# An attention, mixture-of-experts and projection kernel on eight cores: the projection's first block is split, most of it ahead of the last head's closing steps, and its accumulators go from two to four

## What is computed

```
xn  = layernorm(x)                                   # no scale or bias
C_q = xn @ Wq_d + bq_d            # 12 wide
C_kv = xn @ Wkv_d + bkv_d         # 4 wide
q   = C_q @ W_qk + b_qk           # 32 heads x 4
attn = softmax(q . C_kv / sqrt(4))
V   = C_kv @ Wv_u + bv_u          # 32 heads x 128
s   = concat_heads(attn @ V) @ Wo + bo               # 4096 x 4096 projection
f   = xn @ base_W.T + (top-2 of 28 experts, rank-8 LoRA)
out = x + s * silu(f)
```

## Time and profile before

| what | value |
|---|---|
| median of the two timed runs | 1880.22 us (1832.23 and 1928.22) |
| the profiled execution's own time | 1834.81 us |
| its span, slowest core (core 5) | 1832.9 us |
| spans of the eight cores | 1825.0 to 1832.9 us |
| PE busy | 1713.6 us, 93% |
| DVE, ACT, POOL busy | 21%, 38%, 16% |

### The profile page before, as it was taken

How to read it: one execution, slowest core, us unless ns; L and a number is a source line. 1 busy time by engine, 2 the same in 40 slices (tenths; PEclk the granted TensorE clock), 3 DMA queues, 4 the chain that set the end, 5 groups by cost and what they waited for, 6 DMA issues and landing times.

```text
span 1832.9 us, 20080 instructions; the slowest of 8 cores (1825.0 to 1832.9 us)
## 1 busy us (share of the span) xinstructions
PE 1713.6 (93%) x7186; PEld 540.5 (29%) x7186; DVE 386.7 (21%) x482; ACT 694.0 (38%) x680; POOL 295.2 (16%) x377
## 2 busy tenths in 40 slices
PE   3669669999999999999999999999979999999997
PEld 0123112222222222222222222222224444444443
DVE  0065431112112112122112112112121111111111
ACT  3400625555555555554555555555540000000000
POOL 5220200100100100100100100100111222222220
PEclk7679569999999999999999999999989999999999
DMA  9990902522532432432432432442238999999997
GB/s 114 144 109 1 137 2 29 57 30 29 52 36 29 49 39 29 46 41 29 44 44 29 42 45 29 41 46 29 35 38 128 156 169 174 174 166 176 175 162 143
DMA packets 313413, 139.69 MB, mean 76 GB/s; under 512 B 290420, under 2 KB 290564, under 8 KB 313092
## 3 DMA queue, kind: packets, MB, share of 16 engines
q0 software_dynamic: 299168, 96.39, 50.6%
q1 hardware_dynamic: 14152, 42.03, 6.6%
HBM read 201.19 MB, written 25.17 MB: 123 GB/s over the span
## 4 chain that ended last, share of the span: by engine, by line
PE 87%; DMA 8%; DVE 2%; POOL 1%; ACT 1%; issue 1%; DVEq 0%; ACTq 0%; POOLq 0%; SPq 0%
PE arena L923 28%; PE arena L1120 22%; PE arena L948 15%; PE arena L802 15%; DMA xnT<-xT_own 4%; DMA bw_bf<-wo 3%; DMA xst<-xT_oth 1%; PE arena L395 1%; PE arena L407 1%; PE arena L958 1%; PE arena L412 1%; PE arena L403 1%; PE arena L828 1%; PE arena L838 1%; ACT xsq L721 1%
## 5 line engine op out<-in xcount | busy, mean ns | idle before, releaser
L1051 ACT ACTIVATE pbuf<-arena 128x1024 bf16<-128x1024 f32 x512 | 523.4, 1022 | 514.3 <-PE arena L948 510.7
L923 PE MATMUL arena<-xnT,bw_bf 128*128 128x512 bf16 x2048 | 516.4, 382 | 0.0
L1120 PE MATMUL arena<-aoT,bw_bf 128*128 128x512 bf16 x2048 | 446.3, 381 | 9.3 <-DMA bw_bf<-wo 9.0
L948 PE MATMUL arena<-qb,ckv_b 4*128 4x512 bf16 x1024 | 307.6, 379 | 0.0
L802 PE MATMUL arena<-pbuf,kaug 128*8 128x512 bf16 x1024 | 306.1, 379 | 0.6 <-ACT pbuf L1051 0.3
L1120 PEld LDWEIGHTS arena<-aoT,bw_bf 128*128 128x128 bf16 x2048 | 200.3, 98 | 255.7 <-issue 18.1
L446 POOL DMA_DIRECT2D bw_bf<-bwt x128 | 112.6, 901 | 947.9 <-PE arena L802 947.6
L923 PEld LDWEIGHTS arena<-xnT,bw_bf 128*128 128x128 bf16 x2048 | 166.7, 98 | 321.6 <-issue 178.8
L1134 ACT ACTIVATE g_f<-gsl 128x1024 f32<-128x1024 f16 x32 | 33.8, 1057 | 401.2 <-DVE ost L1148 401.2
L1102 POOL DMA_DIRECT2D bw_bf<-wo x128 | 112.3, 899 | 328.6 <-PE arena L1120 328.6
L948 PEld LDWEIGHTS arena<-qb,ckv_b 4*128 4x128 bf16 x1024 | 56.2, 92 | 218.1 <-issue 218.0
(11 more groups left out here) (131 smaller groups left out, 619.5 us busy)
## 6 DMA issues: line engine op xcount, KB each, us to landing
bw_bf<-bwt POOLq DMA_DIRECT2D x128, 256.0 KB, 8.3
bw_bf<-wo POOLq DMA_DIRECT2D x128, 256.0 KB, 8.8
g_f<-xT_own SPq DMA_DIRECT2D x32, 512.0 KB, 7.1
outT<-ost SPq DMA_DIRECT2D x32, 512.0 KB, 4.2
xnT<-xT_own POOLq DMA_DIRECT2D x32, 256.0 KB, 17.1
xst<-xT_oth POOLq DMA_DIRECT2D x32, 256.0 KB, 9.5
gscr<-fsb POOLq DMA_DIRECT2D x32, 256.0 KB, 9.5
gsl<-gscr SPq DMA_DIRECT2D x32, 256.0 KB, 4.8
```

The source lines that it names most:

```text
L923: mm = t.matmul(arena[0:128, FC + c0:FC + c0 + cw], lhsT, rhs, start=st_, stop=sp_, skip_group_check=True)
L948: mm = t.matmul(arena[0:128, PB[p] + c0:PB[p] + c0 + cw], ckv_b[0:KL, kt * 128:(kt + 1) * 128], qbs[h % 2][0:KL, c0:c0 + cw], start=True, ...
L1051: inst = s.activation(pbuf[:, sl * T:(sl + 1) * T], arena[0:128, spair[(h, kt)]:spair[(h, kt)] + T], AF.Exp)
L1120: mm = t.matmul(arena[0:128, PW + c0:PW + c0 + cw], wo_bf[:, (mo % 2) * D + ki * 128:(mo % 2) * D + (ki + 1) * 128], aoT[:, ki * T + c0:ki ...
```

## The change

It does three things.

- A list of four accumulators, `PW4 = [FC, A2C, PB[0], PB[1]]`, replaces the two. Block `mo` uses `PW4[mo % 4]` on PE and on DVE, and waits for `stt` of `mo - 4` in place of `mo - 2`.
- The matmuls of block 0 for ki = 0 to 30 (62 of 64), which read heads 0 to 30 only, are issued in a PE block of their own, behind the last `a2block` and ahead of `emit_bcd` and `emit_up` of head 31. This block waits for the loads of `wo` for block 0 (`wL`, whose value is entered by hand) and for the last `fcp`, since it writes FC. The last two matmuls of block 0 (ki = 31) stay where the whole block was, and wait for the last `uptt`.
- The waits of the first four blocks are set for the last readers of each accumulator.

```diff
+        PW4 = [FC, A2C, PB[0], PB[1]]
+        EV[("wL", 0)] = ("dP0", cnt["dP0"] + 16 * ng)
+
+        @block.tensor
+        def _(t):
+            W(t, ("wL", 0), ("fcp", H - 1))
+            for ki in range(KT - 1):
+                for c0, cw in CH:
+                    t.matmul(arena[0:128, FC + c0:FC + c0 + cw],
+                             bw_bf[:, ki * 128:(ki + 1) * 128],
+                             aoT[:, ki * T + c0:ki * T + c0 + cw],
+                             start=(ki == 0), stop=False, skip_group_check=True)
+
+        @block.tensor
+        def _(t):
             emit_bcd(t, H - 1, 0)
             emit_up(t, H - 1, 1)
...
-                PW = PB[mo % 2]
-                W(t, ("wL", mo), ("stt", mo - 2))
-                if mo < 2:
-                    W(t, ("uptt", H - 1, NCH - 1), *pair_free[mo % 2])
+                PW = PW4[mo % 4]
+                W(t, ("wL", mo), ("stt", mo - 4))
+                if mo == 0:
+                    W(t, ("uptt", H - 1, NCH - 1))
+                    kis = [KT - 1]
+                elif mo == 1:
+                    W(t, ("a2s", H - 1, NCH - 1), ("uptt", H - 1, NCH - 1))
+                    kis = range(KT)
+                elif mo == 2:
+                    W(t, ("uptt", H - 1, NCH - 1), *pair_free[0])
+                    kis = range(KT)
+                elif mo == 3:
+                    W(t, *pair_free[1])
+                    kis = range(KT)
+                else:
+                    kis = range(KT)
                 mm = None
-                for ki in range(KT):
+                for ki in kis:
...
-                                      start=(ki == 0), stop=(ki == KT - 1),
+                                      start=(ki == 0 and mo != 0),
+                                      stop=(ki == KT - 1),
...
-                PW = PB[mo % 2]
+                PW = PW4[mo % 4]
                 vself(v)
                 W(v, ("woT", mo), ("silu", mo), ("out", mo - 2))
```

## The result

| | kernel before | changed kernel |
|---|---|---|
| median of all timed runs | 1837.03 us (18 runs) | 1847.4 us (20 runs) |
| ratio, with 95% interval | 1 | 1.0057 [1.0044, 1.0071] |
| the profiled execution's own time | 1834.81 us | 1841.87 us |
| its span, slowest core | 1832.9 us (core 5) | 1840.3 us (core 6) |
| spans of the eight cores | 1825.0 to 1832.9 us | 1827.0 to 1840.3 us |

So the ratio is 10.4 us (8.1 to 13.0) of added time. It is within 2%, slower as forecast, and two and a half times the 4.0 us of the sum.

What follows compares the result with a forecast made beforehand. PE was taken to bound the kernel, with `wo` loads only just keeping up in the projection. The profiled 1834.8 us plus 4.0 for the exposed tail, all other terms 0, gave 1838.8 us; range 1832.8 to 1846.0.

Steps and rivals of the forecast that it cites:

- step 4: Projection's start: first two `gsl` loads fall beside block 2's `wo` load; taken as 0, between -3.4 and +1.5 us.
- Step 5: PE's idle gap of about 3.1 us behind the early matmuls: clock may halve, 0 to 2.9 us; taken as 0.
- Step 1: Hole before the projection: the 62 early matmuls need the same `wo` loads and start at 1373.25 as before; gain 0.
- Step 2: Head 31's tail (`bcd`, `up`, DVE's four steps) stands behind the 62 matmuls, no longer covered by the load: 4.0 us.
- Step 3: Projection's accumulators and drain: four accumulators worth 0; drain starts 7.3 to 14.1 us behind `uptt`, lag gone within 18 blocks.
- B: Rival: the clock falls in the new gap before block 0's last two matmuls, 1840.3 to 1841.7 us; chance 0.33.
- D: Rival: the projection's drain or `wo` loads fall behind; one to three more early pauses give 1840.3 to 1843.4 us; chance 0.10.

Runs made afterwards that it cites:

- The early loads: Changed kernel with the `wo` loads for block 0 put ahead of the last store of `fsb` on POOL's queue: 0.9939 from 2 runs.
- the tail first: Changed kernel with `bcd` and `up` of head 31 put back ahead of the 62 matmuls, all else kept: 0.9984.
- the early `gsl`: Changed kernel with the first two `gsl` loads waiting for block 1's `wo` load instead of the last `uptt`: 1.0026, again 1.0028.
- The shift alone: Kernel before with its first two `gsl` loads waiting for the end of block 0 instead of the last `uptt`: 1.0035.
- the run with the gap filled alone: Changed kernel with 14 matmuls of no use behind `up`, so PE works through the gap; `gsl` still late: 1.005 from 7 runs.

## Why the prediction was right and wrong

Its main mechanism and its sign were right, its size was not: 1838.8 was said, with 1846.0 as the high end, and 1847.4 measured. The term for the loads in step 4, put at 0, failed: it measured 4.4 us. Step 5 put the clock at 0, where some 2 us were lost on a core.

**Step 1, right.** The early matmuls wait for the same load and fill nothing: 11.38 us of wait on the slowest core, start 12 us behind the start of the last `a2`. The early loads show that this was the point: with the weights there the same 62 matmuls start at the end of `a2`. The load's own time varies more than the prediction allowed: on core 5 the early part started at 1367.53, before the 1369 that was to be a sign against it, 7.2 us behind the end of `a2` (11.4 on core 6). The change isn't needed for that: with the tail first the same wait, from the end of `a2`, was 7.7 to 12.4 us.

**Step 2, right.** The tail in the open: 3.92 us in the profile, 4.0 in the sum, 3.3 us (0.7 to 6.1) left when all else is taken away.

**Step 3, right for the path, off in its parts.** Four accumulators are worth nothing (1.001). The first L1172 came 5.3 us behind `uptt`, not 7.3 to 14.1, since `gsl` took some 3 us on quiet queues, where the earlier trace rows shows it beside eight loads of `wo`. The drain's circle early was 13.5 to 15.4 us on cores 0 and 6, longer than the 13.1 of the sum and mostly than PE's 13.84; it sets nothing, since PE asks for the drain of four blocks earlier. On cores 0 and 2 the profile does put a wait of 2.53 and 1.55 us before block 5 down to DVE's L1172. That block needs the drain of block 1, done some 44 us earlier, so it was another wait that ended there; the load of `wo` is the only other one that the block has.

**Step 4, the term that was mis-sized.** It was put at 0 with +1.5 as its bound, because the load of `g_f` had stood in the place of `gsl` before and "now comes later". It didn't come later by enough. `gsl` landed quickly, the drain followed at once, and `g_f` was issued at 1398.33, still within block 1, so both fell beside the load for block 2. The drain's next transfers moved as well: the store and the third `gsl` were issued at 1408.98 and 1409.47, just behind the load for block 3 (1408.45), where before they stood about 2 us ahead of it (1402.11 and 1402.60, the load at 1404.42, on core 5). Most of the lost time stands ahead of block 3. Which of the moved transfers costs it is not shown, since the early `gsl` moves them all. The bound of +1.5 was one doubled pause. But each load of `wo` is issued only when a block ends and has the 13.84 us of one block to land, so one pause was not the end of it: core 6 paused for a load five times. The shift alone made 1.0035 in the kernel before, and taking it out of the changed one gave 4.4 us back.

**Step 5, the wrong one of two values.** The price was right (2.9 us at most; 2 us in the profile), the chance was not: 5 of 16 stops before, but 5 of 8 cores in this profile and 8 of 8 in its repetition. The stops counted were measured from PE's last matmul of any kind. Here `bcd` and `up` come between the dense work and the idle time, and on 8 of these 13 cores the clock fell 1.1 to 2.2 us behind them, as soon as in the shortest two of the 16 stops or sooner. On the other 5 it fell when the matmuls had been back for about 1.1 us, 4.0 us behind the four thin ones; in 11 of the 16 stops it also fell later than 3.1 us, and the prediction took those as cases without a fall. The rule of the Trainium skill that stood beside the sum (TensorE: Matmul & The Clock Gate, Why this matters for your kernels), to leave no idle gap of about this length between bursts of matmuls, was the better guide, as 13 of 16 cores show: by it the sum would have been up to 1841.7, an estimate.

**The base and the way the cases were put together.** The sum stood on one execution, 1834.8, where the runs of the kernel before have 1836. And B and D were weighed as alternatives with chances for a single core. They happened together, and the time is that of the slowest of eight cores: the shift that costs about 1.4 us on the mean core costs 4.4 on the slowest. The three parts, 3.3 + 4.4 + 1.8 = 9.5 us, make up the 1.0052 of the changed kernel on that chip because they are differences between runs in a row; that is no check of its own. With `gsl` late the clock's part may be smaller, as the run with the gap filled alone (1.005) suggests.

## What to carry to other kernels

Before work is moved ahead of a wait, look whether the moved work waits for the same thing: here the hole belonged to the weights, and the matmuls put into it needed these weights. What had been hidden under the wait then comes out behind it. Moving the load first, and the work after it, turned the same idea from 1.0057 into 0.992. And where transfers only just keep up and the slowest of several cores counts, price a shifted transfer on the worst core, not on the mean.

## What the runs showed of the hardware

The stage's loads have little to spare: with two more loads of 256 KB within one block's 13.84 us, and a later drain, the slowest core waited 5.37 us for block 2, against 1.53 us on the slowest core before, while other cores of the same run didn't wait for it at all. The granted clock fell to half (1.2 GHz) around a stretch of four thin matmuls and 2.9 us of idle time on 13 of 16 cores in two profiles of the changed kernel, on 5 of them about 1.1 us after dense work had begun again. It didn't fall once in two profiles (16 cores) where dense matmuls filled the gap.
